# A graph network kernel: one barrier between stages, a reordered setup, and h and x plus b2 computed in the edge stage and kept with skip as one row a node

## The reference

```python
h = jnp.maximum(_layernorm(x), 0.0)
x = x + _L0_gnn_ref(h, edge_index, edge_attr_4, ...)

def _L0_gnn_ref(x, ...):                 # here x is h
    z = layer_norm(x, ln1_g, ln1_b)
    q, k, v, skip = z @ Wq.T + bq, z @ Wk.T + bk, z @ Wv.T + bv, z @ Wskip.T + bskip
    alpha = (q[dst] * (k[src] + e)) summed over each of 4 heads / sqrt(32)
    out = segment softmax of alpha over dst, times (v[src] + e), segment sum
    beta = sigmoid([out, skip, out - skip] @ Wbeta.T)
    x = x + beta * skip + (1 - beta) * out
    h2 = relu(layer_norm(x, ln2_g, ln2_b) @ W1.T + b1) @ W2.T + b2
    return x + h2
```

## Time and profile before

| | us |
|---|---|
| median of three runs | 4261.69 |
| lowest, highest | 4200.47, 4282.03 |
| the profiled execution | 4272.86 |
| its span | 4271.1 |
| busy: TensorE, weight loads | 2449.4, 1993.8 |
| busy: VectorE, ScalarE, GpSimd | 2146.2, 1716.7, 2380.6 |
| moved by DMA | 479.31 MB, mean 112 GB/s |

### The profile page before, as it was taken

The page is one execution under the profiler, slowest core; times in us unless marked ns, Lnnn a source line. Parts: engine busy times, 40 slices in busy tenths (PEclk is TensorE's granted clock), DMA queues, the critical chain, the costliest instruction groups (busy, mean ns, idle before and its releaser), DMA issues. The chain is left out here.

```text
span 4271.1 us, 56176 instructions
## 1 busy us (share of the span) xinstructions
PE 2449.4 (57%) x13730; PEld 1993.8 (47%) x13730; DVE 2146.2 (50%) x8636; ACT 1716.7 (40%) x4322; POOL 2380.6 (56%) x2380
## 2 busy tenths in 40 slices
PE   0015666677777676757887887888533333343344
PEld 0004666666666666644555555555432232233334
DVE  8982443443444443466666666666311111466567
ACT  7962222232222222236666666667311111333233
POOL 7765444454454444426555555544466665677675
PEclk9998888788888888878888888888755555555555
DMA  6542322232333223243433434433355555345565
GB/s 209 191 149 65 104 89 87 85 108 86 97 101 105 86 89 106 88 112 118 127 113 115 121 113 120 125 103 102 85 118 113 109 120 107 109 123 121 119 134 118
DMA packets 275117, 479.31 MB, mean 112 GB/s; under 512 B 58939, under 2 KB 167880, under 8 KB 274968
## 3 DMA queue, kind: packets, MB, share of 16 engines
q1 hardware_dynamic: 211214, 343.45, 25.4%
q0 software_dynamic: 63424, 133.57, 15.5%
q10 hardware_dynamic: 378, 1.26, 0.1%
HBM read 293.29 MB, written 186.18 MB: 112 GB/s over the span
## 5 line engine op out<-in xcount | busy, mean ns | idle before, releaser
L239 POOL DMA_INDIRECT zs<-z_table,src_col x392 | 372.1, 949 | 667.7 <-PE p_tr L822 486.7
L1380 PE MATMUL p_f<-z_t,w_t 128*128 128x512 f32 x784 | 448.3, 736 | 176.7 <-ACT z_t L1427 119.7
L1768 POOL DMA_INDIRECT aggc<-rows,node_row x392 | 444.0, 1133 | 181.6 <-issue 117.6
L1608 POOL DMA_INDIRECT h2s<-h_table,src_col x392 | 372.0, 949 | 202.0 <-issue 111.1
L1336 POOL DMA_INDIRECT agg<-rows,at_n x392 | 394.9, 1007 | 113.7 <-issue 112.8
L239 POOL DMA_INDIRECT zd<-z_table,dst_col x392 | 371.6, 948 | 125.1 <-issue 121.4
L1689 PE MATMUL p_sum<-h2s,same 128*128 128x129 f32 x784 | 191.7, 420 | 391.1 <-issue 184.9
L1390 PE MATMUL p_f<-w_t,act 128*128 128x128 f32 x3136 | 376.5, 278 | 0.5 <-issue 0.5
L1380 PEld LDWEIGHTS p_f<-z_t,w_t 128*128 128x128 f32 x784 | 182.5, 240 | 415.1 <-issue 378.4
L808 PE MATMUL p_v<-wsk_t,zn_t 128*128 128x129 f32 x784 | 161.9, 340 | 369.5 <-issue 367.3
L1390 PEld LDWEIGHTS p_f<-w_t,act 128*128 128x128 f32 x3136 | 357.5, 192 | 22.2 <-issue 22.2
(11 more groups left out here) (323 smaller groups left out, 6727.8 us busy)
## 6 DMA issues: line engine op xcount, KB each, us to landing
rows<-rows_sb SPq DMA_DIRECT2D x49, 576.0 KB
skip_table<-skip_sb SPq DMA_DIRECT2D x49, 516.0 KB
skipb<-skip_table SPq DMA_DIRECT2D x49, 516.0 KB
h_table<-h2b SPq DMA_DIRECT2D x49, 516.0 KB
rows<-rows_sb SPq DMA_DIRECT2D x49, 516.0 KB
xa<-in_x_dram SPq DMA_DIRECT2D x49, 512.0 KB
z_table<-za SPq DMA_DIRECT2D x49, 512.0 KB
zn<-z_table SPq DMA_DIRECT2D x49, 512.0 KB
```

The lines of the kernel that those rows point to most:

```text
L239: pool.indirect_dma_start(out=to[:, slot, k], out_offset=None, in_=z_table, in_offset=bass.IndirectOffsetOnAxis(ap=col[:, g * G + k:g * G ...
L1380: t_.matmul(p_f1[c][:, :], w1_t[:, c * P:(c + 1) * P], z2_t[:, q].rearrange("p a b -> p (a b)"), start=True, stop=True).then_inc(S["f1_don ...
L1608: pool.indirect_dma_start(out=h2s[:, slot, k], out_offset=None, in_=h2_table, in_offset=bass.IndirectOffsetOnAxis(ap=src_col[:, g * G + k: ...
L1768: pool.indirect_dma_start(out=agg[:, slot, k], out_offset=None, in_=rows1, in_offset=bass.IndirectOffsetOnAxis(ap=node_row[:, g, k:k + 1], ...
```

## The change

1. A stage's semaphores are cleared just before the next stage's block, with no second barrier behind; one full barrier stands at the very end.
2. In the setup two memsets go ahead of stage A's loop, the column transposes use four banks, and the column copies come before the flags.
3. E0 loads x too (`xe`), computes h (`keep_h`, ScalarE) and x + b2 (`add_b2`, VectorE), and stores one row of 385 floats a node: skip and its logit (129), h (128), x + b2 (128). SP's skip store becomes this node store.
4. B loads that row once, instead of x and skip, and has no `h_of`, no copy of the stats and no bias matmul; x + b2 takes the place of x in the sum.
5. In the join a reciprocal moves up. The split of b2 in three parts at the start of E0 goes.

```diff
@@ phase
-            nc.clear_and_free_semaphores(made)
-            nc.all_engine_barrier()
+            spent.extend(made)
+
+        def clear_spent():
+            nc.clear_and_free_semaphores(list(spent))
+            spent.clear()
...
@@ setup, VectorE
-                    nodes_a_vector(dve)
                     chain.mark(v.memset(ones[:], 1.0))
                     chain.mark(v.memset(meta[:], 1.0))
+                    nodes_a_vector(dve)
                     dve.wait_ge(edges_in, 16 * (NB + 2))
...
+                    chain.mark(v.tensor_tensor(cont[:], dstf[:, :, 1], dstf[:, :, 0], ALU.is_equal))
+                    chain.wait()
+                    for b in range(NB):
+                        dve.wait_ge(cols_t, b + 1)
+                        cols = slice(b * RB, (b + 1) * RB)
+                        chain.mark(v.tensor_copy(src_col[:, cols], pbank[at_bank(b)][:, 0:RB]))
+                        chain.mark(v.tensor_copy(meta[:, cols, META - 1], pbank[at_bank(b)][:, P:P + RB]))
+                        v.tensor_copy(dst_col[:, cols], pbank[at_bank(b)][:, P:P + RB]).then_inc(cols_copied, 1)
...
@@ setup, TensorE
                     for b in range(NB):
-                        if b >= 2:
-                            pe.wait_ge(cols_copied, b - 1)
-                        t_.transpose(pbank[b % 2][:, 0:RB], srcf[:, b, :], ident[0:RB, 0:RB])
+                        t_.transpose(pbank[at_bank(b)][:, 0:RB], srcf[:, b, :], ident[0:RB, 0:RB])
...
@@ E0, SP
                             sp.dma_start(zn[:, slot], rows).then_inc(zn_in[slot], 16)
+                            at_least(sp, h_kept, 4 * (g - 1))
+                            at_least(sp, xb_kept, 4 * (g - 1))
+                            hold(sp, held)
+                            rows = x[bass.ds(first_row(g), GR), :].rearrange("(p t) d -> p t d", t=G)
+                            sp.dma_start(xe[:, slot], rows).then_inc(xe_in[slot], 16)
...
                             sp.wait_ge(skip_kept, 4 * g + 4)
+                            sp.wait_ge(h_kept, 4 * g + 4)
                             hold(sp, held)
-                            rows = skip_table[bass.ds(first_row(g), GR), :].rearrange("(p t) d -> p t d", t=G)
-                            sp.dma_start(rows, skip_sb[:, slot]).then_inc(skip_out[slot], 16)
+                            sp.wait_ge(xb_kept, 4 * g + 4)
+                            hold(sp, held)
+                            rows = node_table[bass.ds(first_row(g), GR), :].rearrange("(p t) d -> p t d", t=G)
+                            sp.dma_start(rows, node_sb[:, slot]).then_inc(skip_out[slot], 16)
@@ E0, ScalarE
                     def keep_skip(g, slot, use, n):
                         act.wait_ge(node_skipped, 4 * g + n + 1)
-                        if n == 0:
+                        a.activation(node_sb[:, slot, 2 * n:2 * n + 2, 0:D + 1], p_skip.rearrange("p (t c) -> p t c", t=2), ACT.Copy).then_inc(skip_kept, 1)
+
+                    def keep_h(g, slot, use, u):
+                        if u == 0:
+                            act.wait_ge(xe_in[slot], 16 * (use + 1))
+                            act.wait_ge(norm_set, g + 1)
                             at_least(act, skip_out[slot], 16 * use)
-                        a.activation(skip_sb[:, slot, 2 * n:2 * n + 2], p_skip.rearrange("p (t c) -> p t c", t=2), ACT.Copy).then_inc(skip_kept, 1)
+                        for k in (2 * u, 2 * u + 1):
+                            last = a.activation(node_sb[:, slot, k, D + 1:2 * D + 1], xe[:, slot, k], ACT.Relu,
+                                                bias=norm_e[:, slot, 1, k:k + 1], scale=norm_e[:, slot, 0, k:k + 1])
+                        last.then_inc(h_kept, 1)
...
                             copy_z(*new, 1)
+                            keep_h(*new, 0)
                             copy_v(*new, 0)
...
                             if new:
+                                keep_h(*new, u + 1)
                                 copy_v(*new, u + 1)
@@ E0, VectorE
+                    def add_b2(g, slot, use, u):
+                        if u == 0:
+                            dve.wait_ge(xe_in[slot], 16 * (use + 1))
+                            at_least(dve, skip_out[slot], 16 * use)
+                        v.tensor_tensor(node_sb[:, slot, 2 * u:2 * u + 2, 2 * D + 1:NODE], xe[:, slot, 2 * u:2 * u + 2],
+                                        b2_row[:].unsqueeze(1).broadcast_to([P, 2, D]), ALU.add).then_inc(xb_kept, 1)
...
+                            at_least(dve, h_kept, 4 * (g - 1))
+                            v.tensor_copy(norm_e[:, slot], stats[:, bass.ds(g, 1)].rearrange("p a b c -> p (a b) c")).then_inc(norm_set, 1)
...
                                 count(*new, u)
+                                add_b2(*new, u)
@@ join, VectorE
+                        dve.wait_ge(rooted, 1)
+                        chain.mark(v.reciprocal(row_f, root))
                         dve.wait_ge(turned_ends, 1)
@@ B, SP
-                            rows = x[bass.ds(first_row(g), GR), :].rearrange("(p t) d -> p t d", t=G)
-                            sp.dma_start(x_sb[:, ring], rows).then_inc(x_in[ring], 16)
-                            rows = skip_table[bass.ds(first_row(g), GR), :].rearrange("(p t) d -> p t d", t=G)
-                            sp.dma_start(skip_sb[:, ring], rows).then_inc(skip_in[ring], 16)
+                            rows = node_table[bass.ds(first_row(g), GR), :].rearrange("(p t) d -> p t d", t=G)
+                            sp.dma_start(node_sb[:, ring], rows).then_inc(node_in[ring], 16)
@@ B, TensorE
-                        t_.matmul(p_f2[q][:, :], ones3[:], b2_parts[:], start=True, stop=False)
                         for k in range(4):
                             for c in range(4):
-                                last = t_.matmul(p_f2[q][:, k * D:(k + 1) * D], act1[:, q, c, k * P:(k + 1) * P], w2_t[:, c], start=False, stop=(k == 3 and c == 3))
+                                last = t_.matmul(p_f2[q][:, k * D:(k + 1) * D], act1[:, q, c, k * P:(k + 1) * P], w2_t[:, c], start=(c == 0), stop=(c == 3))
@@ B, ScalarE
-                        if fetch:
-                            h_of(*fetch, range(G))
```

More of the change, by code:

```diff
@@ L46 @@
 ROW0 = MSG + H2
+NODE = 3 * D + 1
 DV = D + H
@@ L666, in build @@
             zn, zn_t = t("zn", [P, 2, G, D]), t("zn_t", [P, 2, 2, P])
-            skip_sb = t("skip_sb", [P, 2, G, D + 1])
+            node_sb = t("node_sb", [P, 2, G, NODE])
+            xe, norm_e = t("xe", [P, 2, G, D]), t("norm_e", [P, 2, 2, G])
+            xe_in = [s(f"e0_xe_in{a}") for a in range(2)]
+            norm_set, h_kept, xb_kept = s("norm_set"), s("h_kept"), s("xb_kept")
             p_alpha, p_back, p_ea = p_small[0:G * H, 0:P], p_small[:, P:P + 2 * G * H], p_small[:, 256:256 + P]
@@ L1145, in _ @@
                     chain = Chain(dve, e0_step)
-                    chain.mark(v.memset(ones3[:], 1.0))
                     chain.mark(v.memset(metag[:], 0.0))
-                    for row, n, parts, times in ((b2_row[:], D, b2_parts, 4),):
-                        chain.step(v.tensor_copy(part1[:, 0:n], row))
-                        chain.step(v.tensor_tensor(rest[:, 0:n], row, part1[:, 0:n], ALU.subtract))
-                        chain.step(v.tensor_copy(part2[:, 0:n], rest[:, 0:n]))
-                        chain.step(v.tensor_tensor(rest[:, 0:n], rest[:, 0:n], part2[:, 0:n], ALU.subtract))
-                        chain.step(v.tensor_copy(part3[:, 0:n], rest[:, 0:n]))
-                        chain.step(v.tensor_scalar(mixed3[:, 0:n], part1[:, 0:n], ident[0:3, 0:1], None, ALU.mult))
-                        chain.step(v.scalar_tensor_tensor(mixed3[:, 0:n], part2[:, 0:n], ident[0:3, 1:2], mixed3[:, 0:n], ALU.mult, ALU.add))
-                        chain.step(v.scalar_tensor_tensor(mixed3[:, 0:n], part3[:, 0:n], ident[0:3, 2:3], mixed3[:, 0:n], ALU.mult, ALU.add))
-                        for j in range(times):
-                            chain.mark(v.tensor_copy(parts[:, j * n:(j + 1) * n], mixed3[:, 0:n]))
-                        chain.wait()
                     dve.wait_ge(wea1_done, 64)
@@ L1230, in join @@
                             v.tensor_tensor(joined[:, b, 0:MSG], joined[:, b, 0:MSG], part[:, b], ALU.add).then_inc(joined_s, 1)
-                        dve.wait_ge(rooted, 1)
-                        chain.step(v.reciprocal(row_f, root))
                         chain.step(v.tensor_tensor(root, row_f, row_f, ALU.mult))
@@ L1405, in _ @@
                     a = nc.scalar
-                    def h_of(g, slot, use, ring, lap, tiles):
-                        if 0 in tiles:
-                            act.wait_ge(x_in[ring], 16 * (lap + 1))
-                            act.wait_ge(S["tab_ready"], g + 1)
-                            at_least(act, S["base_ready"], g - WAYS + 1)
-                        for k in tiles:
```

(4 more changed lines are left out.)

50 lines of the change are left out of this document (21 added, 29 removed).

## The result

| | us |
|---|---|
| before, on the chip of the comparison: median of four | 4257.64 |
| after, same chip: median of four (3886.28 to 3927.94) | 3919.68 |
| ratio | 0.924, 95% interval 0.918 to 0.930 |
| predicted | 4251, range 4170 to 4325 |

The kernel after is 7.6% faster there, outside the predicted range. On another Trainium2 chip the same two kernels turned out otherwise: 3260.39 before, 3540.23 after, against that chip's own runs of the kernel before a ratio of 1.087 (interval 1.084 to 1.091). Both numbers need an explanation, and the larger part of this text is on them.

The account below looks back on a forecast made before the run. It took TensorE, at a clock below full speed, to bound E0 and B. Terms -2.4 - 4.4 + 24 - 30 + 2 (B's larger first loads) = -11 gave 4262 against 4272.86 profiled, so a 4251 us median; range 4170 to 4325.

Parts of the forecast that it names:

- Setup (-4.4): Setup: memsets moved and index copies earlier let the first gather go at 288.8 instead of 293.15, saving 4.4 us.
- barriers (-2.4): Stage boundaries: four of five barriers lose their second half, 0.6 us each, saving 2.4 us.
- The added wait in E0 (+24): E0: the first relu waits for the larger node store and delays v, 0.5 us a group, +24 us (0 to +53).
- the slower rival: E0: the node store paces ScalarE, 2.5 us a group, +120 us instead of +24, total 4347; chance 0.12.
- v is needed by about 1023: E0, one step: TensorE needs copied v only by about 1023, so the delay is 0 to 1.1 us a group.
- Added work in E0 (nothing): E0: ScalarE's relus (155 us in all) and VectorE's adds (1.7 us a group) fit into existing waits, costing nothing.
- B (-30): B: TensorE loses two bias matmuls a group, about 0.31 us each, saving 30 us (0 to 38).
- with both shorter, the smaller saving counts: B: ScalarE's relus and TensorE's bias matmuls lie on chains covering each other, so only the matmuls' 30 us count.
- B gets out of its stalls: B: ScalarE's 3.2 us a group come in full, 127 us more, total 4124, or half, 4187; chance 0.18.
- B at 21 or below: ScalarE was the bound: B: sign that the forecast is wrong; steps of 21 us or less would mean ScalarE was the bound.
- Its line on the clock: B, in the faster rival: mean clock 0.87 means about a quarter at the lower level, worth up to 13% of 1130 us.
- the longer wait in E0 hurts: E0: by the skill's rule that idle gaps lower TensorE's clock, the longer wait would hurt; no size given.

Follow-up runs that it names:

- before2: The kernel before, unchanged, traced on a chip where it runs at about 3255 us; 3260.39 us, ratio 1.0015.
- after2: The kernel after, unchanged, on another chip than the comparison's; 3540.23 us, ratio 1.087 to the kernel before there.
- a_split: The kernel after with skip and (h, x + b2) in separate tiles and stores, relus and adds later in E0; 3209.46 us, ratio 0.986 to the kernel before.
- before: The kernel before, unchanged, as profiled on the chip of the comparison; span 4271.1 us.
- after: The kernel after, unchanged, as profiled on the chip of the comparison; span 3926.1 us.
- b_nobias: The kernel before without B's bias matmuls, b2 left out of the output, relus kept; 4013 and 4152 us, against a median of 4229 before.
- a_both: The kernel after with bias matmuls and eight relus a group (constants for scale and bias) put back in B; 3924 and 3976 us, against 4229 before.
- b_nohof: The kernel before without ScalarE's relus in B, x added in place of h, bias matmuls kept; 4168 and 4163 us, against 4229 before.
- E1: Not a run: a stage of the kernel after B, timed together with the last stage; 1226.3 us before, 1236.1 after, on the chip of the comparison.

## Why the prediction was wrong, by its steps

- **Setup (-4.4): right; barriers (-2.4): not seen whole.** The first gather went at 288.82 (288.8 said), and E0 begins 4.4 us sooner, the barrier's share included. Counted from the end of a stage's own barrier, at the four boundaries, SP's next transfer is now issued 0.5 to 0.9 us sooner, but GpSimd's first gather only 0.06 to 0.24 us, about 0.5 in all.
- **The added wait in E0 (+24): the mechanism right, its price wrong on both kinds.** Relu(0) starts 8.95 us after the rows' store (9 to 10.5 said). On the chip of the comparison it cost nothing: E0 and join gave 41 us. On the quick kind it cost 344 us, beyond even the slower rival's 120. The failed step is "v is needed by about 1023": I read the need from the times of the weights and the skip product in one execution, but in that step the clock had fallen, and TensorE was late itself. That the wait costs nothing on the slow kind is more than the slack read there explains, and stays open. Undisturbed there is no such slack: in `before2` ScalarE waits for TensorE ahead of v, 1.5 us at a time (259.6 us in 169), and copies it as soon as it is there, and in `after2` the 5.7 us that v comes later come back as 5.4 us of TensorE. The Trainium skill (DMA: Bandwidth & Descriptors, "Anatomy of one DMA") was weighed there with its 2 us; the section is on DMAs that GpSimd issues, and this store is SP's. 8.2 us from the issue of the node store to the relu cannot tell it from a slower transfer, and the price did not hang on it.
- **Added work in E0 (nothing): right where it stands late.** `a_split` has it all, placed later, and loses at most 10.5 us (1033.4 against 1022.9).
- **B (-30): wrong, -308.9.** The failed step is "with both shorter, the smaller saving counts", a sum of two chains of work, in a stage whose time was not the sum of its work. By the quick kind the work removed is worth 50.1 us (860.2 to 810.1), 20 more than said, 16 of them since a bias matmul costs 0.47 us and not the 0.31 between the starts of the records. The other 259 us are slow phases that ended: they cost 284 us of B in `before` (1144.0 less 860.2) and 25 in `after` (835.1 less 810.1).
- **The rival "B gets out of its stalls" (4124 or 4187, chance 0.18) had the sign and place.** The size was 6.5 us a group and not 3.2, since I priced only ScalarE's work; and my reading "B at 21 or below: ScalarE was the bound" is false, as `b_nobias`, with all relus in B, has steps of 16.2 at 4013.
- **Its line on the clock** ("worth up to 13% of 1130 us", 147) was too low: the lateness ahead of each fall is not in the record. The Trainium skill (TensorE: Matmul & The Clock Gate, "HAM oscillation") says that idle gaps of TensorE bring the lower clock back. The quick kind agrees: with the gap of 5.4 us in each group of E0 the granted clock is 0.88, without it 1.00. On the slow kind "the longer wait in E0 hurts" did not come true, with 0.84 to 0.86 against 0.83 before; but there TensorE's own waits ahead of its skip matmuls did not grow (338.5 us after, 367.3 before), so this doesn't speak against the rule.

That most of B's gain comes from slow phases ending is shown by the stage's time on both kinds and by the count of clock falls. What starts a phase, why it needs a certain kind of chip, and which part of the change ended them is not: taking out the bias matmuls was enough in one execution of `b_nobias`, and putting them back with half of the relus' cost did not bring the phases back in `a_both`, so the single load or the new E0 may have a share.

**What to use.** On the quick kind `a_split` beats both kernels (3209 against 3254 and 3540). On the slow kind it is 3979, against 4256 before and 3861 after. It beats the kernel before on both kinds; the kernel after does so on the slow kind alone, and by more.

## What to carry to other kernels

Time an engine's need from a stretch in which it is not itself stalled: a slack read in a disturbed stage is no slack on a chip that isn't disturbed. A tile that is stored whole makes its first writer wait for the whole store; keep what is on the path (here the skip copies) in a small tile of its own, and put work with slack behind the copies that others wait for, not ahead of them (`a_split` did both at once). And where one program runs 4250 us on one chip and 3255 on another, a ratio from one chip is not yet the effect of the change.

## What the hardware did that I had not expected

- Two kinds of chip for one program: 4156 to 4282 and 3247 to 3271 us, none between in 34 runs of the kernel before. E0 and join take 1589 or 1023 us, B 1144 or 860, E1 and C 1226 or 1061.
- Results of TensorE that come 2.0 to 4.8 us after the record's end, the first two while the clock reads 1.00, and a fall of its record to 0.55 only from 2524 on (2520.50 and 2521.38 recorded; 2522.54, 2523.98 and 2526.14 seen).
- Two lengths of step, about 17 and about 22 us, in one execution of `b_nohof`.
- A slow phase costs about 6.5 us of B: 44, 37 and 45 falls of the clock went with 284, 248 and 292 us more.
- On the slow kind, E0 got shorter where ScalarE was held ahead of v (1483 to 1547 us against 1583 to 1608).
- A relu of 128x128 with constants starts 0.21 us after the last, with scale and bias as operands 0.40.
